# Feed-forward in pairs of chunks, its first layer as three rounded passes

## The reference, cut to what matters

```python
    def _L1_ffn_ref(x, fc1_w, fc1_b, fc2_w, fc2_b):
        ...
        ll, lh, hl, hh = _haar_dwt2(x)
        ll_up = _interp_linear_last(ll, c)
        h = jax.nn.gelu(jnp.einsum('bfc,hc->bfh', ll_up, fc1_w) + fc1_b, approximate=False)
        ll_new = jnp.einsum('bfh,oh->bfo', h, fc2_w) + fc2_b
        return _haar_idwt2(ll_new, lh, hl, hh)
    ...
    t = t + _L1_ffn_ref(_ln_t(t), L1_ffn_fc1_w, L1_ffn_fc1_b, L1_ffn_fc2_w, L1_ffn_fc2_b)
```

## Time and profile before

| what | value |
|---|---|
| median of 3 runs | 5421.32 us (5418.6 to 5423.04) |
| profiled execution, own time | 5428.35 us |
| profiled execution, span | 5426.6 us |
| busy in the span: TensorE / VectorE / ScalarE / GpSimd | 97% / 72% / 45% / 46% |
| feed-forward phase, first transfer to the end of the span | 4981.4 to 5426.6 us |
| its first-layer matmuls | from 4999.50 us |
| its part of the chain that ended last, by line | L2514 40.0%, L2483 38.3%, L2498 10.5%, L2530 5.5% |

### The profile page before, as it was taken

One profiled execution on the slowest core, in us unless ns is written; L12 is line 12 of the kernel. 1 busy time (PEld: TensorE's weight loads), 2 busy tenths in 40 slices (PEclk: granted clock), 3 DMA queues, 4 the chain that ended last, 5 costly groups with the idle time before them and its releaser, 6 DMA issues. The chain is left out here.

```text
span 5426.6 us, 88825 instructions
## 1 busy us (share of the span) xinstructions
PE 5245.8 (97%) x26936; PEld 3653.4 (67%) x26936; DVE 3927.7 (72%) x6063; ACT 2458.1 (45%) x4678; POOL 2491.1 (46%) x1381
## 2 busy tenths in 40 slices
PE   9999999997999999999998999999989999988999
PEld 6777655554555555555556777777667777765999
DVE  6666566666999999999995666666635666665887
ACT  4444478784344334333334555555532222211555
POOL 0000044443999999999995554555301111111332
PEclk9999999998999999999999999999999999998999
DMA  3222167775444444444446666666533333423443
GB/s 109 88 88 71 42 195 218 220 220 167 150 151 148 150 151 148 150 151 148 149 134 181 198 203 195 196 203 196 163 106 99 103 113 107 120 82 93 122 123 113
DMA packets 349116, 782.55 MB, mean 144 GB/s; under 512 B 43433, under 2 KB 147845, under 8 KB 339460
## 3 DMA queue, kind: packets, MB, share of 16 engines
q1 hardware_dynamic: 326596, 703.91, 43.9%
q10 hardware_dynamic: 22400, 77.08, 4.0%
HBM read 420.49 MB, written 360.38 MB: 144 GB/s over the span
## 5 line engine op out<-in xcount | busy, mean ns | idle before, releaser
L890 POOL TENSOR_TENSOR co_prod<-co_cross 111x512 f32<-111x512 f32 x448 | 849.8, 1897 | 0.0
L824 ACT ACTIVATE co_y_out<-co_y_ps 112x512 f32<-112x512 f32 x448 | 268.0, 598 | 927.3 <-PE co_y_ps L770 922.6
L887 POOL TENSOR_TENSOR co_prod<-co_direct 111x512 f32<-111x512 f32 x448 | 577.0, 1288 | 203.1 <-PE co_y_ps L770 115.1
L864 DVE TENSOR_TENSOR co_direct<-co_v_ps,co_spec 111x1024 f32<-111x1024 f32 x448 | 543.7, 1214 | 91.8 <-PE co_v_ps L135 87.5
L1974 POOL TENSOR_TENSOR at_t<-at_t,at_p_bias 112x1024 f32<-112x1024 f32 x56 | 137.7, 2472 | 900.1 <-DMA at_t<-t_tiles 900.1
L866 DVE TENSOR_TENSOR co_cross<-co_v_ps,co_spec 111x1024 f32<-111x1024 f32 x448 | 541.9, 1210 | 0.0
L135 PE MATMUL co_v_ps<-co_v_high,co_col_fwd_high 112*111 112x512 f32 x896 | 506.1, 565 | 1.5 <-DVE co_cross L866 1.4
L768 PE MATMUL co_y_ps<-co_prod,co_col_inv 111*112 111x512 f32 x896 | 458.2, 592 | 0.0
L770 PE MATMUL co_y_ps<-co_prod,co_col_inv 111*112 111x512 f32 x896 | 457.5, 592 | 0.1
L844 DVE TENSOR_TENSOR co_v_low<-co_v_in,co_v_high 112x1024 fp32r<-112x1024 f32 x224 | 372.5, 1663 | 0.0
L135 PE MATMUL co_v_ps<-co_v_low,co_col_fwd_high 112*111 112x512 f32 x896 | 354.3, 395 | 0.0
(11 more groups left out here) (269 smaller groups left out, 14135.3 us busy)
## 6 DMA issues: line engine op xcount, KB each, us to landing
v_rows<-pr_rows_out SPq DMA_DIRECT2D x56, 1792.0 KB, 8.2
co_v_in<-v_rows SPq DMA_DIRECT2D x448, 224.0 KB
y_rows<-co_y_out SPq DMA_DIRECT2D x448, 224.0 KB
mx_y_in<-y_rows SPq DMA_DIRECT2D x224, 448.0 KB, 5.4
kr_x_in<-x SPq DMA_DIRECT2D x56, 448.0 KB, 3.7
kern_rows<-kr_rows_out SPq DMA_DIRECT2D x28, 896.0 KB, 4.7
pr_x_in<-x SPq DMA_DIRECT2D x112, 224.0 KB
mx_x_in<-x SPq DMA_DIRECT2D x56, 448.0 KB, 5.3
```

What stands on the lines that cost most here:

```text
L824: nc.scalar.activation(y_out[:, b, :], y_ps[b % 2][:2 * SIDE, :], ACT.Copy).then_inc(y_ready, 1)
L864: nc.vector.tensor_tensor(direct[b % 2][:], v_ps[b % 2][:POINTS, :], spec[i][:, :2 * WIDE], ALU.mult).then_inc(real_terms, 1)
L887: nc.gpsimd.tensor_tensor(prod[b % 2][:, :WIDE], direct[b % 2][:, :WIDE], direct[b % 2][:, WIDE:], ALU.subtract).then_inc(real_ready, 1)
L890: nc.gpsimd.tensor_tensor(prod[b % 2][:, WIDE:], cross[b % 2][:, :WIDE], cross[b % 2][:, WIDE:], ALU.add).then_inc(combined, 1)
```

## The change

A step now takes a pair of chunks, `q`; `e` is its parity, `u` the chunk within it.

- The first layer's weights and the low band are split into rounded high and rest (`fc1_high`, `fc1_low`; `low_parts`), the weights once by ScalarE and VectorE, the low band of each pair by a second ScalarE copy and a subtraction on VectorE (`low_part`). `hidden` calls `product` with 448 columns, so a block is three passes over both chunks. `low` itself stays for the change instruction.
- The second layer stays unrounded, with 448 columns for both chunks. The blocks come in groups of four: hidden 4 to 7, second 0 to 3, low band of the next pair (both chunks, 16 instructions), second 4 to 7, the next pair's hidden 0 to 3, eight transposes.
- ScalarE's gelus and VectorE's change instruction span both chunks.
- `t2`, `n2` and `base` have four buffers, two pairs of two. Tokens are loaded two pairs ahead. GpSimd writes `base` of pair `q` when the output of pair `q - 2` is written.
- VectorE's order in step `q`: normalise chunk 0 of pair `q + 1`, output of chunk 0 of pair `q - 1`, the same two for chunk 1, `low_part` of `q + 1`, change of `q`.
- SP's and GpSimd's loops are written out; the other engines loop over two pairs.

```diff
-        fc1 = T.sb("fc1", [128, HIDDEN])
+        parts = ("high", "low")
+        fc1 = [T.sb(f"fc1_{part}", [128, HIDDEN], F32R) for part in parts]
...
-        t2 = [T.sb(f"t2{u}", [TILE, TILES, CH]) for u in range(2)]
+        t2 = [[T.sb(f"t2{e}{u}", [TILE, TILES, CH]) for u in range(2)] for e in range(2)]
...
-        n2 = [T.sb(f"n2{u}", [TILE, TILES, CH]) for u in range(2)]
-        base = [T.sb(f"base{u}", [TILE, TILES, CH]) for u in range(2)]
+        n2 = [[T.sb(f"n2{e}{u}", [TILE, TILES, CH]) for u in range(2)] for e in range(2)]
+        base = [[T.sb(f"base{e}{u}", [TILE, TILES, CH]) for u in range(2)] for e in range(2)]
         sums = [T.sb(f"sums{u}", [TILE, TILES, CH // 2]) for u in range(2)]
-        low = [T.sb(f"low{u}", [128, PAIRS_T]) for u in range(2)]
-        hid = T.sb("hid", [128, NB, PAIRS_T])
-        change = T.sb("change", [128, CHUNK])
+        low = [T.sb(f"low{e}", [128, CHUNK]) for e in range(2)]
+        low_parts = [[T.sb(f"low{e}_{part}", [128, CHUNK], F32R) for part in parts] for e in range(2)]
+        hid = T.sb("hid", [128, NB, CHUNK])
+        change = T.sb("change", [128, 2, CHUNK])
...
+        def all_steps(eng, step):
+
+            step(0, 0)
+            with eng.Fori(1, PAIRS // 2) as s:
+                step(s * 2 - 1, 1)
+                step(s * 2, 0)
+            step(PAIRS - 1, 1)
...
+                def load(q, u):
+                    sp.dma_start(t2[q % 2][u][:], d["t2_tiles"][2 * q + u]).then_inc(loaded[q % 2][u], 16)
...
+                for q in range(PAIRS):
+                    if q + 2 < PAIRS:
+                        for u in range(2):
+                            sp.wait_ge(base_ready, 2 * q + u + 1)
+                            load(q + 2, u)
+                    for u in range(2):
+                        sp.wait_ge(out_ready, 2 * (2 * q + u + 1))
+                        sp.dma_start(d["out"][2 * q + u], out[u][:]).then_inc(stored[u], 16)
...
-                with pool.Fori(0, PAIRS - 1) as s:
+                for q in range(PAIRS):
                     for u in range(2):
-                        pool.wait_ge(out_ready, 2 * (2 * s + u + 1))
-                        add(s + 1, u)
+                        pool.wait_ge(n2_ready, 2 * q + u + 1)
+                        if q >= 2:
+                            pool.wait_ge(out_ready, 2 * (2 * (q - 2) + u + 1))
+                        nc.gpsimd.tensor_tensor(base[q % 2][u][:], t2[q % 2][u][:], n2[q % 2][u][:], ALU.add).then_inc(base_ready, 1)
...
-                def hidden(s, u, m):
-                    nc.tensor.matmul(hid_ps[m % FB][:, :PAIRS_T], fc1[:, m * 128:(m + 1) * 128], low[u][:],
-                                     start=True, stop=True).then_inc(hid_mm, 1)
...
+                def hidden(e, m):
+                    product(nc, hid_ps[m % FB][:, :CHUNK], [w[:, m * 128:(m + 1) * 128] for w in fc1],
+                            [part[:] for part in low_parts[e]], start=True, stop=True).then_inc(hid_mm, 1)
...
+                def low_band(q):
+
+                    pe.wait_ge(sums_ready, 2 * q + 2)
+                    at_least(pe, low_ready, q)
+                    at_least(pe, low_copied, q)
+                    for u in range(2):
+                        for t in range(TILES):
+                            mm = nc.tensor.matmul(low_ps[:, u * PAIRS_T + t * SIDE:u * PAIRS_T + (t + 1) * SIDE], sums[u][:, t, :],
+                                                  pair_tok[:], start=True, stop=True)
+                    mm.then_inc(low_mm, 1)
...
-                        last = nc.tensor.matmul(new_ps[:, :PAIRS_T], fc2[:, m, :], hid[:, m, :], start=m == 0, stop=m == NB - 1)
+                            at_least(pe, change_ready, q)
+                        mm = nc.tensor.matmul(new_ps[:, :CHUNK], fc2[:, m, :], hid[:, m, :], start=m == 0, stop=m == NB - 1)
                         if m == NB - 1:
-                            last.then_inc(new_mm, 1)
+                            mm.then_inc(new_mm, 1)
 
                     for m in range(FB, NB):
-                        second(m - FB)
-                        hidden(s, u, m)
-                    if after:
-                        low_band(*after)
-                    for m in range(NB - FB, NB):
+                        pe.wait_ge(hid_ready, q * NB + (m - FB + 1))
+                        hidden(e, m)
+                    for m in range(FB):
                         second(m)
-                    if after:
-                        first_hidden(*after)
-                    pe.wait_ge(change_ready, g + 1)
-                    pe.wait_ge(out_ready, 2 * g)
-                    for t in range(TILES):
-                        last = nc.tensor.transpose(up_ps[u][:TILE, t * 128:(t + 1) * 128], change[:, t * TILE:(t + 1) * TILE],
-                                                   ident[:])
-                    last.then_inc(up_mm, 1)
+                    if not last(q):
+                        low_band(q + 1)
+                    for m in range(FB, NB):
+                        second(m)
+                    if not last(q):
+                        first_hidden(q + 1, 1 - e)
+                    pe.wait_ge(change_ready, q + 1)
+                    at_least(pe, out_ready, q * 4)
+                    for u in range(2):
+                        for t in range(TILES):
+                            mm = nc.tensor.transpose(up_ps[u][:TILE, t * 128:(t + 1) * 128], change[:, u, t * TILE:(t + 1) * TILE],
+                                                     ident[:])
+                    mm.then_inc(up_mm, 1)
...
-                def take_low(s, u):
-                    act.wait_ge(low_mm, 2 * s + u + 1)
-                    buffer_used(act, change_ready, s, u)
-                    nc.scalar.activation(low[u][:], low_ps[:, :PAIRS_T], ACT.Copy).then_inc(low_ready, 1)
-
-                def front(s, u):
-                    take_low(s, u)
-
-                def step(now, after):
-                    s, u = now
-                    g = 2 * s + u
-                    act.wait_ge(new_mm, g)
+                def take_low(q, e):
+                    act.wait_ge(low_mm, q + 1)
+                    at_least(act, change_ready, q - 1)
+                    nc.scalar.activation(low[e][:], low_ps[:, :CHUNK], ACT.Copy).then_inc(low_copied, 1)
+                    nc.scalar.activation(low_parts[e][0][:], low_ps[:, :CHUNK], ACT.Copy).then_inc(low_high, 1)
+
+                def step(q, e):
+                    at_least(act, new_mm, q)
                     for m in range(NB):
-                        act.wait_ge(hid_mm, g * NB + m + 1)
-                        nc.scalar.activation(hid[:, m, :], hid_ps[m % FB][:, :PAIRS_T], ACT.Gelu,
+                        act.wait_ge(hid_mm, q * NB + (m + 1))
+                        nc.scalar.activation(hid[:, m, :], hid_ps[m % FB][:, :CHUNK], ACT.Gelu,
...
+                def low_part(q, e):
+                    dve.wait_ge(low_high, q + 1)
+                    nc.vector.tensor_tensor(low_parts[e][1][:], low_ps[:, :CHUNK], low_parts[e][0][:].bitcast(F32), ALU.subtract
+                                            ).then_inc(low_ready, 1)
...
+                        if not first(q):
+                            finish(q - 1, 1 - e, u)
+                    if not last(q):
+                        low_part(q + 1, 1 - e)
+                    dve.wait_ge(new_mm, q + 1)
+                    at_least(dve, up_mm, q)
+                    dve.wait_ge(low_copied, q + 1)
+                    twice = [128, CHUNK, 2]
+                    nc.vector.scalar_tensor_tensor(out=change[:].rearrange("p u (t r) -> p (u t) r", r=2),
+                                                   in0=new_ps[:, :CHUNK].unsqueeze(2).to_broadcast(twice), scalar=fc2_bias[:, 0:1],
+                                                   in1=low[e][:].unsqueeze(2).to_broadcast(twice), op0=ALU.add, op1=ALU.subtract
+                                                   ).then_inc(change_ready, 1)
...
+                for i in range(2):
+                    dve.wait_ge(fc1_high, i + 1)
+                    nc.vector.tensor_tensor(fc1[1][:, i * 512:(i + 1) * 512], up_ps[i][:], fc1[0][:, i * 512:(i + 1) * 512].bitcast(F32),
+                                            ALU.subtract).then_inc(fc1_ready, 1)
+                low_part(0, 0)
```

More of the change, by code:

```diff
@@ L2409, in ffn_phase, with at_least, first, last @@
         stats_in, weights_in = T.sem("stats_in"), T.sem("weights_in")
[L2412 to L2424, removed]
+        def at_least(eng, sem, value):
+            if not (isinstance(value, int) and value <= 0):
+                eng.wait_ge(sem, value)
+        def all_steps(eng, step):
[4 more added lines that the diff above has]
+            step(PAIRS - 1, 1)
+        def first(q):
+            return isinstance(q, int) and q == 0
+        def last(q):
+            return isinstance(q, int) and q == PAIRS - 1
         with nc.Block() as block:
@@ L2432, in _ @@
```

(36 more changed lines are left out.)

107 lines of the change are left out of this document (41 added, 66 removed).

## The result

| | before | after |
|---|---|---|
| median (range), 6 runs each | 5419.96 us (5413.36 to 5423.04) | 5444.53 us (5441.85 to 5450.86) |
| profiled execution: own time, span | 5428.35, 5426.6 us | 5450.58, 5448.8 us |
| feed-forward phase in it: first transfer to the end | 445.2 us | 470.9 us (from 4977.86) |

The ratio is 1.0052, 95% interval 1.0042 to 1.0061 (the two medians alone give 1.0045): the change makes the kernel 0.5% slower. 5412.3 us was predicted, with a range of 5392 to 5430. The difference of the medians, 24.6 us, is that of the two phases, 25.7 us within what two executions differ by.

What follows compares the result with a forecast made beforehand. A chain of TensorE matmuls was taken as the bound; start 5004.0 + 14.7 + 26 x 14.50 + 11.9 + end 10.0 gave 5417.6, 9.0 us under the 5426.6 span, so 5412.3 against the median; range 5392 to 5430.

Steps and rivals of the forecast that it cites:

- The failed step: SP's queue: both token loads leave behind the second store; the first needed at 1.55 lands near 0.8, cover 0.75 us.
- time 0: The moment in each step where the last second-layer matmul of a pair has been streamed; other times count from it.
- the late load: Store and loads served by turns: load lands about 2.2 after time 0, wanted at 1.55; 17 us more, 5429; chance 0.11.
- The clock: TensorE busy 95% of each pair, its clock falls; three parts in a hundred lost are 12 us, 5424; chance 0.05.
- the collision: GpSimd's addition holds VectorE's second normalise before the low band; TensorE stands still about 0.74 us in each pair.
- The chain over both sums: Low band waits for both next chunks' sums through VectorE and GpSimd: period 14.50 us instead of 14.99; chance 0.60.
- TensorE's own work: First layer 4.87, second layer 6.02, low band 1.87, transposes 0.98 us: 13.74 a pair, taken as 13.76, against 14.99.
- First layer: On TensorE, 8 blocks of three rounded 448-column passes, 0.203 us each: 4.87 us a pair against 6.06, 2.44 for four blocks.
- VectorE: Per pair: change instruction 1.145 us, low-part subtraction 0.625, first normalise unhindered at 1.38, second held near 3.5.
- Table load: ScalarE's table load at the gelu happens once in two pairs, with slack, so the extra 0.21 us goes.
- Start: Low band waits for the second chunk and the weights' low part: first layer starts at 5004.0, 4.5 us late.
- End: After the last second layer: longer change, more transposes, a second finish and the later store, 10.0 us against 7.36.

Runs made afterwards that it cites:

- the early loads: Changed kernel with each token load issued a pair earlier, one behind each store, instead of both behind the second store: 5405.36 us, ratio 0.9979 to the kernel before.
- the order without idle time: Changed kernel with VectorE normalising both chunks of the next pair before finishing both of the last, loads unchanged: 5385.34 us, ratio 0.9947 to the kernel before.
- the unrounded run: Changed kernel with both normalises before both outputs on VectorE and first layer back to unrounded 448-column products: 5418.26 us, ratio 1.0003 to the kernel before.
- the profiled run: Changed kernel with early loads and an unused 448-column VectorE instruction heading each step: 5440.95 us median of ten runs, ratio 1.0032; this run among three at 5417 to 5421.

## Why the prediction was wrong, point by point

**The failed step** is that on the loads: "First in first out, the load needed at 1.55 lands near 0.8. Cover 0.75 us." The order of issue, the order of landing and the 3.3 us of advance were right (5218.65, time 0 being at 5222.00). The time was mis-sized: 4.15 us from issue to landing were counted, 5.7 were measured (5.9 in the median of the steady pairs), so the load landed at 2.37, not at 0.8, and instead of a cover of 0.75 us there was a lateness of 0.8. Two things are in that. Right behind a store and with nothing behind it a load takes 4.9 us: it lands 1.9 after the store, not 1.3, and in the pair shown above the three transfers together move at 221 to 315 GB/s in the microseconds from 5219 to 5224, not at the 348 of one microsecond in the earlier trace rows. And the second load right behind it, counted at nothing, makes its last pieces 1.0 us later. The earlier trace rows held a warning: a store of the same size took 3.3 us to land, not 1.3.

**The rival that came true** was the late load, at 0.11: 2.2 us after time 0, 0.65 late, 17 us, 5429. That a late load binds is confirmed, and its landing came near (2.37). Its reason for the lateness is not: the transfers land in order, the store at 3.4 us and not with the loads, so that the number was met by luck. Its price was short, because it was priced alone. The clock was a second rival, at 0.05, priced alone too. They are one chain: a late load makes TensorE idle longer than the collision does, that brings the clock down, and the slow pair gives the load its time back, whereupon it starts over. 14.8 us of idle time is the 17 of the rival; the 22.2 us of the clock come on top. The earlier trace rows show that 97.23 busy of 100 kept the clock; the early loads, with 329.99 of 340, kept it too. Idle for 0.42 us in 14.3 cost only itself; idle for 1.1 to 2.3 us in every second pair or so, in the kernel after, it brought a fall in eleven of the fourteen pairs that began so; and for 1.39 us in 15.3, in every pair, in nearly every one.

**The chain over both sums** was right. With the loads early the pair takes 14.28 us and TensorE's own work 13.59 (the order without idle time): a loss of 0.69, where 0.74 was predicted. TensorE's own work was counted 0.17 high: eight transposes take 0.87 us (5204.89 to 5205.76 in the unrounded run), not 0.98, and sixteen low-band matmuls start 1.72 us ahead of the second layer, not 1.87.

**First layer**: 0.203 predicted; 0.20 apart, four blocks in 2.46 (2.44). **VectorE**: change 1.15 (1.145), low part 0.62 (0.625), one normalise 1.38 and one 3.42 (3.53). **Table load**: one at the gelu in the whole phase, where one in two pairs had been expected; why is not shown.

**Start**: the first layer starts at 5003.73 (5004.0), but by luck, since this execution's phase began 3.5 us earlier than that of before. From the first transfer it is 25.9 us against 18.1, 7.8 late where 4.5 was counted; with the loads early 24.2, 6.1 late. The row of the low band gives half of the reason:

```profile
4998.38 3.57 PE L2497 MATMUL ff_low_ps<-ff_pair_tok,ff_sums 112*128 112x56 f32 x16 [4.52 <-DVE ff_fc_low L2640]
```

Sixteen matmuls at half clock take 3.57 us, not 2.05. Most of the rest was there earlier: the factors that normalising needs are ready 11.5 us behind the first transfer, where it was 10.2 before, and the issue of the eight transfers ahead of them took 4.9 us instead of 3.6. **End**: 10.3 us after the last second layer (10.0).

**Altogether**: with the loads out of the way the forecast of 9.0 us below the kernel before would have been met: 5405.36 is 10.0 below the 5415.34 timed beside it. (Against the 5412.3 itself it is 7 us low, but 6 of these are the kernel before, which the sum took at 5421.32.) Within that, errors cancel: the 25 pairs are 5.5 us shorter than counted, the start is 1.6 later. The sum was good but for the loads and for the clock that they bring down, which was priced at nothing in the sum, and these two set the sign.

## What to carry to other kernels

A transfer issued right behind another lands later by more than its bytes suggest (here 4.9 us instead of 3.5), and one issued right behind it in turn delays its last pieces (5.9): read the time from issue to landing from rows with the same neighbours, and give the one that is needed first a place without neighbours. Before a chain that TensorE waits for, do what feeds it first and what only drains it later: the order within one VectorE step was worth 57 us of the phase here with no work changed. And where a change leaves TensorE regularly idle, price the clock with the idle time, not as a separate risk: here its falls cost 22.2 us, the idle time that brought them 14.8.

## What the runs showed of the hardware

- A load of 448 KB lands 3.5 us after its issue when the store ahead was issued 2.5 us before, 4.9 right behind a store, 5.9 right behind a store with another load right behind it; that other load lands after 6.5. The 16 landings of each transfer come in the order of issue, and the store ahead keeps its 3.3 to 3.4 us.
- A fall of TensorE's granted clock to half lasts 3.4 us, sometimes 6.8, and one of 3.4 costs 1.7. In the steady stretch, idle times of 0.42 us in each 14.28 us never brought one, of 1.39 in 15.26 nearly always. Of 0.93 in 14.79 they brought one in the profiled run; slower runs of the same kernel had a lower mean clock.
- Rounded passes keep their price per column when they are halved: 0.20 us apart for 448 columns, 0.11 for 224.
- GpSimd won the pair against VectorE in the rows of before, although recorded 0.07 us later; in the kernel after it is recorded 0.07 us earlier (5212.83, 5212.90), and wins too.
